# First head's stack through DRAM, and attention's loop over groups written out

## The reference, cut to what matters

```python
def _L1_conv_ref(x, w_qkv, b_qkv):          # R = 32 heads of d = 8 channels
    xr = x.reshape(B, C, HW).transpose(0, 2, 1).reshape(B, HW, R, d).transpose(0, 2, 1, 3)
    qkv = jnp.einsum('brnd,ed->brne', xr, w_qkv) + b_qkv
    q, k, v = jnp.split(qkv, 3, axis=-1)
    attn = jnp.einsum('brnd,brmd->brnm', q, k)
    attn = jax.nn.softmax(attn, axis=0)     # over the 8 images
    out = jnp.einsum('brnm,brmd->brnd', attn, v)
```

## Time and profile before

| | us |
|---|---|
| median of 3 runs | 686.96 (685.99 to 689.05) |
| the profiled execution | 684.06 |
| its span | 681.9 |
| TensorE busy (share of the span) | 580.0 (85%) |
| VectorE busy | 476.0 (70%) |
| ScalarE busy | 327.6 (48%) |
| GpSimd busy | 383.2 (56%) |
| attention, from the first L1074 to the start of the last L363 | 120.7 to 431.9 |

### The profile page before, as it was taken

One profiled execution on the slowest core, in us unless ns is written; L12 is line 12 of the kernel. 1 busy time (PEld: TensorE's weight loads), 2 busy tenths in 40 slices (PEclk: granted clock), 3 DMA queues, 4 the chain that ended last, 5 costly groups with the idle time before them and its releaser, 6 DMA issues.

```text
span 681.9 us, 13628 instructions
## 1 busy us (share of the span) xinstructions
PE 580.0 (85%) x4548; PEld 367.2 (54%) x4549; DVE 476.0 (70%) x835; ACT 327.6 (48%) x707; POOL 383.2 (56%) x237
## 2 busy tenths in 40 slices
PE   3777795899999997999999999499974799999954
PEld 2444363655555554665555555278863366666633
DVE  3434575799999998699999999566558334334325
ACT  2334466467676765467667676234321133333310
POOL 1000046399999998479999999422001466666520
PEclk9777879699999999589999999789985699999985
DMA  9711115623112221112221100000002223222239
GB/s 303 295 33 32 32 70 149 254 85 104 70 63 70 70 69 68 31 47 71 67 67 60 62 29 1 1 0 1 32 32 65 64 79 95 86 86 92 72 100 309
DMA packets 30520, 56.58 MB, mean 83 GB/s; under 512 B 8362, under 2 KB 22339, under 8 KB 29443
## 3 DMA queue, kind: packets, MB, share of 16 engines
q1 hardware_dynamic: 25715, 38.97, 17.7%
q0 software_dynamic: 3744, 10.39, 4.9%
q10 hardware_dynamic: 1008, 6.49, 2.4%
HBM read 37.84 MB, written 17.40 MB: 81 GB/s over the span
## 4 chain that ended last, share of the span: by engine, by line
POOL 38%; PE 35%; issue 10%; DVE 7%; ACT 4%; DMA 3%; SPq 1%; POOLq 1%; ACTq 0%
POOL e_ring L363 38%; PE ps L1246 10%; PE ps L1262 5%; PE ps L989 2%; PE ps L1057 2%; PE ps L1178 2%; PE ps L1013 2%; DVE stats L639 2%; PE ps L1200 2%; PE ps L1002 1%; PE ps L1136 1%; PE ps L1191 1%; PE ps L1238 1%; SPq L340 1%; PE ps L1254 1%
## 5 line engine op out<-in xcount | busy, mean ns | idle before, releaser
L363 POOL TENSOR_TENSOR e_ring<-e_ring,x_hat 128x1024 f32<-128x1024 f32 x128 | 272.7, 2134 | 47.2 <-ACT x_hat L538 35.9
L528 ACT ACTIVATE e_ring<-ps 128x1024 f32<-128x1024 f32 x128 | 131.2, 1025 | 105.4 <-PE ps L1083 105.4
L747 DVE TENSOR_REDUCE m_bf<-ps 128x128 bf16<-128x1024 f32 x128 | 155.5, 1215 | 16.6 <-PE ps L1074 16.6
L754 DVE TENSOR_REDUCE x_hat<-e_ring 128x128 f32<-128x1024 f32 x128 | 154.8, 1210 | 6.4 <-ACT e_ring L528 6.3
L1074 PE MATMUL ps<-q_stack,k_stack 72*128 72x128 bf16 x1024 | 142.4, 325 | 13.3 <-DMA k_stack<-e_ring 9.7
L1074 PEld LDWEIGHTS ps<-q_stack,k_stack 72*128 72x128 bf16 x1024 | 106.5, 135 | 40.5 <-issue 40.1
L1083 PE MATMUL ps<-m_bf,ident_neg 128*128 128x512 bf16 x256 | 82.5, 406 | 14.1 <-DVE m_bf L747 6.7
L1097 PE MATMUL ps<-e_ring,v_slot 128*32 128x128 f32 x2048 | 87.7, 289 | 3.6 <-POOL e_ring L363 3.6
L1097 PEld LDWEIGHTS ps<-e_ring,v_slot 128*32 128x32 f32 x2048 | 50.9, 110 | 59.8 <-issue 53.4
L1246 PE MATMUL ps<-w_sb,e_ring 128*128 x156 | 75.2, 605 | 0.3 <-issue 0.3
L396 POOL DMA_INDIRECT pair_rows<-scratch,slot_y x39 | 38.5, 987 | 39.4 <-DVE scratch L951 37.6
(11 more groups left out here) (149 smaller groups left out, 702.4 us busy)
## 6 DMA issues: line engine op xcount, KB each, us to landing
q_stack<-qk_parts SPq DMA_DIRECT2D x31, 288.0 KB
k_stack<-qk_parts SPq DMA_DIRECT2D x93, 96.0 KB
w_sb<-in_w13T_dram ACTq DMA_DIRECT2D x2, 2048.0 KB, 10.0
qk_parts<-e_ring SPq DMA_DIRECT2D x2, 1536.0 KB, 5.1
qk_parts<-scratch SPq DMA_DIRECT2D x2, 1536.0 KB, 16.3
x_res<-in_x_dram SPq DMA_DIRECT2D x8, 256.0 KB, 4.0
w_sb<-in_w2T_dram ACTq DMA_DIRECT2D x2, 1024.0 KB, 15.8
token_rows<-work SPq DMA_DIRECT2D x4, 512.0 KB, 3.0
```

Of the source, the lines that this page charges most:

```text
L363: nc.gpsimd.tensor_tensor(ev, ev, view(x_hat, CH + (u % RS) * P, [[0, BQ], [1, P], [0, 2]]), ALU.mult).then_inc(norm_done, 1)
L528: nc.scalar.activation(e_ring[:, u % ER, :], score_banks(v), ACT.Exp).then_inc(exp_done, 1)
L747: nc.vector.tensor_reduce(m_bf[:, u % 2], by_position(score_banks(v).rearrange("p a c -> p (a c)")), AXY, ALU.max).then_inc(max_done, 1)
L754: nc.vector.tensor_reduce(s_sum[:, u % 2], by_position(e_ring[:, u % ER, :]), AXY, ALU.add).then_inc(sum_done, 1)
```

## The change

Head 0 of group 0 is loaded like the other heads, by `load_stack(0, 0)` out of DRAM, after the wait for the stores of the lower channels; the six direct loads and ScalarE's wait for them go, and TensorE's count for head 0 becomes that of the others. And `attention_steps` writes units 16 to 127 straight, with constants in all waits, instead of a loop of two passes and a last group.

```diff
             for u in range(UPG):
                 step(u, u, u, 0, lambda k: k <= u)
-            with eng.Fori(0, (NG - 2) // SLOT) as t:
-                for j in range(1, SLOT + 1):
-                    for u in range(UPG):
-                        step(t * (SLOT * UPG) + (j * UPG + u), j * UPG + u, u, t * SLOT + j, lambda k: True)
-            for u in range(UPG):
-                step((NG - 1) * UPG + u, (NG - 1) * UPG + u, u, NG - 1, lambda k: True)
+            for U in range(UPG, UNITS):
+                step(U, U, U % UPG, U // UPG, lambda k: True)
             for u in range(LAG):
                 step(UNITS + u, UNITS + u, u, NG, lambda k: k > u)
...
-            for a in range(PARTS):
-                rows_a = slice(a * PARTS * D, (a + 1) * PARTS * D)
-                q_src = parts[0][0:D, 0]
-                k_src = bass.AP(parts[0].tensor, 2 * H * UW + (PARTS + a) * T, [[H * ER * UW, D], [0, PARTS], [1, T]])
-                sp.dma_start(q_stack[rows_a, 0, :], q_src).then_inc(stack_in[0], 16)
-                sp.dma_start(k_stack[rows_a, 0, :], k_src).then_inc(stack_in[0], 16)
             for n in range(2):
                 sp.wait_ge(parts_out[n], 16)
-            for i in range(1, HPG):
+            for i in range(HPG):
                 load_stack(0, i)
...
                 elif U == 2:
-                    act.wait_ge(stack_in[0], 2 * PARTS * 16)
                     for s in range(2):
                         act.wait_ge(parts_out[s], 16)
...
                 if u % 4 == 0:
-                    pe.wait_ge(stack_in[i], (g + 1) * ((PARTS + 1) * 16) + (2 * 16 if i == 0 else 0))
+                    pe.wait_ge(stack_in[i], (g + 1) * ((PARTS + 1) * 16))
```

More of the change, by code:

```diff
@@ L251, in later_than @@
             return not isinstance(U, int) or U >= k
-        assert (SLOTS - 7) % XR == 0 and (NG - 2) % SLOT == 0 and UPG % ER == 0
+        assert (SLOTS - 7) % XR == 0 and UPG % ER == 0
         block = ctx.enter_context(nc.Block())
```

## The result

| | us |
|---|---|
| median of the changed kernel, 4 runs | 677.01 (676.27 to 682.71) |
| median of the kernel before, 4 runs beside it | 686.48 (683.09 to 689.05) |
| ratio | 0.9869, interval 0.9825 to 0.9913 |
| the profiled execution, before and after | 684.06 and 677.54 |
| predicted | 668.0, range 662 to 675 |

The change makes the kernel faster, by about 9 us (1.3%), where 18.5 were forecast. The direction was right and half of the size was missing. All ratios here are estimated from the runs of the fast state, so they need not equal the quotient of the two medians shown. The first view is GpSimd's timeline around the places where it breaks into a new group, as in the earlier trace rows; L353 is the line that was L363.

The account below looks back on a forecast made before the run. VectorE was taken to set attention's pace, GpSimd just behind. 12.05 us (loop) plus 5.4 (first head's stack) made 17.45 off 684.06, so 666.6; 669.5 with the runs' excess; 668.0 was taken, range 662 to 675.

Parts of the forecast that it names:

- The loop: Attention, unit 64: TensorE's jump back stalls it and lowers the clock; straight code saves 12.05 us (3.6 jump, 8.4 clock).
- ScalarE's and VectorE's jumps: Attention loop: these jumps vanish too but lie in the shadow of TensorE's wait, so they bring nothing extra.
- VectorE's pace: Steady attention: VectorE sets a unit's pace, 2.26 us, with two reductions of 1215 and 1210 ns; a group takes 36.71.
- The stack: Attention's start: head 0's stack loaded through DRAM lets TensorE start 5.4 us earlier, all reaching the end.
- the landing of its loads: Head 0's four loads land 4.0 us after the last issue, at 115.3; bounds 2.3 to 7.3 us.
- The landing of the stores: Before head 0's loads: the lower channels' stores take 5.1 us to land, the second at 109.0.
- The clock at the start: Attention's start: low stretch assumed about like the old one, no gain; full clock would give an estimated 2 us.
- the first rival: Start brings nothing, through slow DRAM round or longer low clock (5.6 us lost): 672.0, up to 675; chance 0.13.
- The choice of 668.0: Whole kernel: median taken as 668.0, not 669.5, since the runs' excess may partly be a longer low stretch at the jump.
- the second (678.7): Attention loop: the stall is not the jump and straight code has it too; only the start's gain remains, 678.7; chance 0.05.
- the first L1074 after 118 us: Attention's start: TensorE's first scores matmul, expected at 115 us instead of 121; after 118 would show the prediction wrong.
- The third (straight code that is fetched late): Attention: TensorE runs out of written-out code, 12.05 us per stall; 690.7 with two, 702.8 with three; chance 0.04.

Follow-up runs that it names:

- the loop alone: Kernel before with only attention's loop over groups written out, head 0 still loaded straight from e_ring: 675.3 us beside 681.49, ratio 0.9892.
- the stack alone: Changed kernel with the loop over groups put back, so only the first head's loading differs from the kernel before: 678.28 us, ratio 0.9971.

## Why the prediction was wrong, and where it was right

**The loop: the mechanism was right, the term too large.** The stall on TensorE's jump, its place at unit 64, the lost clock behind it, and the 36.71 us of all groups afterwards came as forecast. The first failing step is the one that entered 12.05 us, taken from one profiled execution, into a sum for the median. The prediction itself split it into "3.6 us is the jump and 8.4 is the clock". The first is nearly fixed (3.2 to 3.6 us in three profiles), the second was the dearest of three (0.8, 3.3 and 8.5 us). With the mean of 7.6 us instead of 12.05 the sum is 4.4 us smaller; the loop alone measured 6.2 us in the medians.

The rows before already held the warning: low stretches of 13.7 and 23.9 us after pauses of 9.7 and 3.6 us, the longer one after the shorter pause. A term that is mostly such a stretch has a range of its own, and mine had none.

**ScalarE's and VectorE's jumps** had no visible stall of their own to hide. The term of zero was right for another reason than the one given.

**VectorE's pace** was read rightly from the breaks (2.26 us per unit), but the 1215 and 1210 ns beside it add up to 2.43. The reductions start 1.13 us apart in the steady stretch, so their records overlap; the mean duration is not the pace.

**The stack: the second failing step is the landing of its loads.** The prediction took 4.0 us from the last issue to landing, "since the four loads together are bigger than one of x but share the queue with nothing before them". It measured 6.4 to 7.6 over the six profiles with these loads, 7.1 in the mean: about the far end of the bounds (7.3), for which the prediction gave 2.1 us of gain. The 4.0 us came from a load of x that is laid out over 128 partitions; the load of q has a broadcast of 3 outermost, and the queue's share at its end was that of 3 engines. Size and neighbours in the queue were weighed, the shape was not. The landing of the stores was smaller in effect: SyncE went on 5.2 to 5.9 us after the second store's issue instead of 5.1. Counting both, the pause fell from 9.7 to 9.9 us (three profiles with the direct loads) to 7.6 to 8.9 (six with the change's loads), about 1.8 us in the mean instead of 5.4, and the stack alone gained 0.3% in the runs, not clear of none.

**The clock at the start** stayed low as assumed, for 10.2 to 23.9 us. To take no gain from it was right. It was also a cost that moves by 3 us from one execution to the next, which was in the first rival and not in the forecast.

**The choice of 668.0** instead of 669.5 leaned on the hope that part of the excess of the runs over the profile came from a longer low stretch at the jump. The profiled stretch was the longest of three, so the median run probably had less to gain from the jump than the profile, not more. This step, the 4.4 us of the loop and the 3.6 of the stack together are 9.5 us; the miss is 9.0.

With 7.6 for the loop and 1.8 for the stack the sum is 9.4 us off 686.48, which is 677.1; 677.01 was measured. That is luck, nearer than either number deserves: the 7.6 is a mean of three. Of the rivals, the second (678.7) came nearest in number, by chance: its mechanism, a stall that the straight code has too, did not occur. The first (the start brings nothing, 672.0) described half of what happened. Of the signs of being wrong that the prediction named, one came: the first L1074 after 118 us. The third (straight code that is fetched late) did not occur: no "issue" wait of TensorE in attention in any kernel with its program written out.

## What to carry to other kernels

When a term is read from one execution, split it into what the program fixes and what the clock adds, and give the second a range from the other low stretches of the trace. Before costing a DMA by size, look at the outermost dimension of both its sides: with a broadcast of 3 outermost in a 288 KB load the set of loads took 8.8 to 10.0 us from first issue to landing, and the same bytes in another order of rows took 5.7 and 6.1. A jump is worth removing where a trace shows a stall on it: here that was the engine with the longest body, TensorE, and the jumps of the two engines with shorter ones cost nothing visible.

## What the runs showed of the hardware

- A jump back over 48 units of TensorE's program stalled it for 3.58, 3.39 and 3.18 us; the jump of ScalarE and VectorE over the same units did not stall them visibly (reductions 1.13 us apart through it).
- After these three stalls the granted clock stayed at half for 23.9, 10.2 and 3.4 us, while TensorE did the same work. It fell 2.4, 4.6 and 3.5 us after TensorE had stopped, in the last two cases when TensorE was already at work again. Three executions do not tell what sets the length. After the pause at attention's start it was 10.2 to 27.3 us over the profiles in which nothing filled the pause.
- With 3 outermost in q's load the 16 DMA engines had a busy share of 0.17 to 0.20 in the backlog, and 0.18 with head 0's loads alone; with 24 outermost the queue moved 192 instead of 126 GB/s between 115 and 120 us.
- ScalarE has stops of up to 3.6 us in the expert stage in some executions, in the kernel before as well. The stage then takes 117.9 to 120.3 us instead of 115.2 to 116.7. Their cause is open.
